# Layer 0 attention of a four-layer network: row normalisations, q and v's chunks in another order on VectorE and TensorE

## The reference

```
x = x + tanh(g_xattn[0]) * _L0_xattn_ref(_layernorm(x, axis=-1), ctx_1024, wq, bq, wk, bk, wv, bv, ln_g, ln_b, ...)

q = visual_tokens @ wq.T + bq
res = q
k = top_k_report_tokens @ wk.T + bk
v = top_k_report_tokens @ wv.T + bv
attn = softmax(einsum('bhqd,bhkd->bhqk', qh, kh) * d ** (-0.5), axis=-1)
out = einsum('bhqk,bhkd->bhqd', attn, vh)
out = _layernorm(res + out, ln_g, ln_b)
return _kan_linear(out, base_w, spline_w, spline_scaler, _grid())   # silu(out) @ base_w.T + b_splines(out) @ scaled_sw.T
```

## Time and profile before

| | us |
|---|---|
| median of 3 runs | 2769.6 (2768.28 to 2770.19) |
| the profiled execution, its own time | 2766.18 |
| its span in the trace, first to last instruction | 2764.4 |
| layer 0's attention stage ends at about | 412.9 |
| PE busy in the span | 2617.9 (95%) |
| DVE / ACT / POOL busy | 1547.1 / 1296.0 / 642.0 |

### The profile page before, as it was taken

The page is one execution under the profiler, slowest core; times in us unless marked ns, Lnnn a source line. Parts: engine busy times, 40 slices in busy tenths (PEclk is TensorE's granted clock), DMA queues, the critical chain, the costliest instruction groups (busy, mean ns, idle before and its releaser), DMA issues. The chain is left out here.

```text
span 2764.4 us, 56714 instructions
## 1 busy us (share of the span) xinstructions
PE 2617.9 (95%) x19818; PEld 1981.6 (72%) x19818; DVE 1547.1 (56%) x4177; ACT 1296.0 (47%) x3610; POOL 642.0 (23%) x626
## 2 busy tenths in 40 slices
PE   6999978999999999989899998999998999989998
PEld 4777756666666666656677766999995777768887
DVE  4777856555555555535787874333235887742222
ACT  4777743343434334331567663333335777732222
POOL 0666661000000000000444431222221111013232
PEclk9999989999999999999999999999999999999999
DMA  3000002000000000010000006999991000059897
GB/s 119 17 23 18 12 2 109 13 13 8 13 7 13 7 13 7 1 34 1 20 18 19 23 7 244 324 334 327 323 326 46 24 18 24 7 201 312 303 312 224
DMA packets 91811, 267.57 MB, mean 97 GB/s; under 512 B 25068, under 2 KB 50804, under 8 KB 77268
## 3 DMA queue, kind: packets, MB, share of 16 engines
q1 hardware_dynamic: 74356, 242.53, 25.4%
q0 software_dynamic: 13632, 18.62, 3.2%
q10 hardware_dynamic: 3616, 3.67, 0.4%
HBM read 248.13 MB, written 16.65 MB: 96 GB/s over the span
## 5 line engine op out<-in xcount | busy, mean ns | idle before, releaser
L825 PEld LDWEIGHTS a_full_ps<-ident,a_probs 112*125 112x125 f32 x2688 | 369.9, 190 | 122.6 <-issue 59.8
L1926 PEld LDWEIGHTS m_banks<-m_x_inT,m_w 128*128 128x128 f32 x3824 | 435.1, 192 | 15.2 <-issue 13.5
L1926 PE MATMUL m_banks<-m_x_inT,m_w 128*128 128x128 f32 x3824 | 442.2, 276 | 1.4 <-ACT m_x_inT L1997 0.9
L936 ACT ACTIVATE a_probs<-a_masked,a_negmax 112x375 f32<-112x375 f32 x512 | 305.4, 598 | 287.7 <-DVE a_negmax L1151 287.7
L825 PE MATMUL a_full_ps<-ident,a_probs 112*125 112x112 f32 x2688 | 417.5, 281 | 16.7 <-ACT a_pT L943 5.6
L1177 DVE COPY a_pT<-a_full_ps 125x448 f32<-125x448 f32 x448 | 277.4, 621 | 233.9 <-PE a_full_ps L825 231.9
L725 PE MATMUL a_full_ps<-attention_room 128*125 128x256 f32 (+1 forms) x960 | 330.0, 472 | 9.6 <-ACT a_qT L926 3.7
L717 PE MATMUL a_full_ps<-attention_room 128*128 128x375 f32 x896 | 325.0, 491 | 13.8 <-PEq L1769 8.6
L1151 DVE CUSTOM_DVE_ANT_0 a_masked<-a_sc_ps,a_mask_add 112x375 f32<-112x375 f32 x512 | 249.7, 544 | 33.2 <-PE a_sc_ps L812 32.0
L936 ACT ACTIVATE a_probs<-a_sc_ps,a_negmax 112x375 f32<-112x375 f32 x384 | 216.6, 575 | 89.4 <-DVE a_negmax L1157 89.3
L843 PEld LDWEIGHTS a_o_ps<-a_pT,a_v 125*32 125x32 f32 (+1 forms) x5376 | 165.2, 118 | 127.0 <-issue 98.7
(11 more groups left out here) (253 smaller groups left out, 3473.3 us busy)
## 6 DMA issues: line engine op xcount, KB each, us to landing
m_w<-in_L2f_w SPq DMA_DIRECT2D x105, 1024.0 KB, 6.4
m_w<-in_L3f_w SPq DMA_DIRECT2D x72, 768.0 KB, 5.9
attention_room<-in_ctxT SPq DMA_DIRECT2D x64, 375.0 KB, 3.1
m_w<-in_L3f_w SPq DMA_DIRECT2D x36, 640.0 KB
m_b<-in_L2f_b SPq DMA_DIRECT2D x35, 128.0 KB, 8.0
p_rows<-normed SPq DMA_DIRECT2D x16, 224.0 KB, 6.2
attention_room<-in_L0x_spline_wT SPq DMA_DIRECT2D x1, 2048.0 KB, 10.5
net_room<-in_L1f_w SPq DMA_DIRECT2D x2, 1024.0 KB
```

Source lines behind the costliest of these rows:

```text
L825: mm = pe.transpose(full_ps[0:KT, bank_of["turn", i, k], (j % 4) * S:(j % 4 + 1) * S], probs[:, i % 2, a, t * KT:(t + 1) * KT], ident[0:S, ...
L936: act.activation(probs[:, i % 2, a, 0:SK], src, ACT.Exp, bias=negmax[:, m:m + 1], scale=-1.0 if mask else 1.0, accum_out=rowsum[:, par, n: ...
L1926: mm = pe.matmul(ab_ps[:, (par * FC + f) % RING, i * SLOTS:(i + 1) * SLOTS], w[:, par, c, f * P:(f + 1) * P], x_inT[:, c, :], start=(c == ...
```

## The change

Only layer 0's attention stage changes, and there only orders; no instruction is added or removed. (1) In the table, q stands directly behind k, ahead of turn 1, and so in the bank of xT; (2) `rest` stands ahead of v's second chunk, and qtok last: v's second and third chunk get the banks of `lnt` and of turn 2, and qtok that of `kan`. (3) On VectorE resn stands in front of silu and the maxima, and the variance in front of the copy of turn 2. (4) `norm_apply`, `net_settle` and `norm_net.apply` stand between `norm_stats` and `update`.

```diff
 CYCLES = {
-    0: [[[("xT",)], [("k", 0)], [("q", 0), ("oback",)], [("v", 0, 0), ("k", 1)]],
-        [[], [], [("kan",), ("lnt",)], [("v", 1, 0), ("qtok",), ("v", 2, 0), ("rest",)]]],
+    0: [[[("xT",)], [("k", 0), ("q", 0)], [("oback",)], [("v", 0, 0), ("k", 1)]],
+        [[], [], [("kan",), ("lnt",)], [("rest",), ("v", 1, 0), ("v", 2, 0), ("qtok",)]]],
...
                         kan_residual(t - 1)
+                    if exists(t - 1):
+                        kan_variance(t - 1, 1 - par)
                     if exists(t):
                         copy_turn(t, 0, 2)
-                    if exists(t - 1):
-                        kan_variance(t - 1, 1 - par)
                     if exists(t - 2):
                         kan_cube(t - 2, 1)
+                    if exists(t - 1):
+                        kan_early(t - 1, 1 - par, 1)
+                    if exists(t - 2):
                         kan_silu(t - 2)
-                    if early(t - 3):
-                        net_settle(t - 3)
                     for group in ahead(t, par, 1):
                         row_max(*group)
-                    if exists(t - 1):
-                        kan_early(t - 1, 1 - par, 1)
...
                         norm_stats(t + 2)
+                    if early(t - 3):
+                        net_settle(t - 3)
+                    if exists(t + 2):
+                        norm_apply(t + 2)
+                    if early(t - 3):
+                        norm_net.apply(dve, t - 3, t - 3)
                     if exists(t - 2):
                         update(t - 2, full_ps[:, bank_of[("kan",)], :])
                     if exists(t):
                         copy_turn(t, 1, 2)
-                    if exists(t + 2):
-                        norm_apply(t + 2)
                     copies(t, par, 1, 3)
                     if exists(t - 2):
                         row_stats(t - 2)
-                    if early(t - 3):
-                        norm_net.apply(dve, t - 3, t - 3)
```

## The result

In ten runs of each on one chip the changed kernel took 2776.36 us (2770.38 to 2777.81), the kernel before 2770.09 (2768.28 to 2771.67): a ratio of 1.0021, 95% interval 1.0011 to 1.0030. It is slower, by 6.3 us or 0.2%; the forecast was 9.3. The profiled execution of the changed kernel took 2777.27 us, its span 2775.4, 11.0 more than the span of before. That is more than the 6.3 of the medians, since the profiled execution of before (2766.18) was quicker than each of the ten that give its median.

What follows compares the result with a forecast made beforehand. A VectorE and GpSimd cycle of 22.17 us a turn, over TensorE's 21.26, was to bind the changed kernel; 0.75 + 5.3 + 1.4 + 1.95 - 0.1 = +9.3 on 2769.6 gave 2778.9 us, range 2766 to 2786.

Steps and rivals of the forecast that it cites:

- The full turn: Full turns: a VectorE and GpSimd cycle of 22.17 us, 0.48 more than before, giving +5.3 over 12 turns.
- they take SBUF at 175.79 ... and the square is held until 176.26: Lines 1080 and 195 hold GpSimd's square, making its chain 0.33 us later; bounds 0 and 0.5.
- late resn: One turn before was 22.04 us long by a late resn; that 0.34 goes, leaving 5.3 of 5.8.
- q and v: TensorE's waits for q's copies and x's update shrink by 0.13 and 0.30, 0.43 us a turn, to 21.26.
- New waits: TensorE waits some 0.9 us a turn, before pv and silu's product; the late copy gives back about 0.12 at v's third chunk.
- The start: Turn 0: the copy of turn 2 comes behind line 1080 and v's third chunk waits: +0.75 us, bounds 0 and 1.1.
- Turn 15: pv waits for a copy that now follows held line 1211 and the variance: +1.4 us, bounds 0.5 to 2.
- Turn 16: Silu stands behind a held resn, and with it TensorE's 778: +1.95 us, bounds 0 to 2.2.
- Turn 17: One norm less stands in front of the cubes: -0.1 us.
- (c): Rival: `add_bases` gets SBUF between resn and silu, holding silu; +24 us more, 2803; chance 0.06.
- (a): Rival: TensorE stays the bound, the chain has unseen slack; sum -1.5 us, 2768.1, no change; chance 0.27.
- (d): Rival: the 0.9 us waits cost TensorE its clock in many turns; 9 us more, 2788; chance 0.06.

Runs made afterwards that it cites:

- e10_short_cube: Kernel before with the change's new table, VectorE's old order, and GpSimd's cube of near2's second half cut to one element: turn 21.77 us, ratio 0.9994.
- e16_before_act_square: Kernel before with ScalarE instead of GpSimd making the square of near2's second half: turn 21.71 us, ratio 1.0004.
- e13_after_short_cube: Changed kernel with GpSimd's cube of near2's second half cut to one element: turn 21.24 us, ratio 0.9979.
- e14_act_square: Changed kernel with ScalarE instead of GpSimd making the square of near2's second half: turn 21.24 us, ratio 0.9997.
- e15_act_square_tail: Changed kernel with ScalarE making the square of near2's second half, and VectorE's old order in turns 15 to 17: turn 21.24 us, ratio 0.9984.
- e1_table: Kernel before with only the change's new table, VectorE's order as before: turn 21.78 us, ratio 1.0014.
- e4_norms_back: Changed kernel with lines 1080 and 195 put back behind the update: turn 21.77 us, ratio 1.0006.
- e3_norms_only: Changed kernel with copy, variance, silu, maxima and resn back in the old order; new table and norms ahead stay: turn 21.78 us, ratio 1.0013.
- e2_vector: Changed kernel with the old table, VectorE's order the new one: turn 21.88 us, ratio 1.0025.
- e7_delay: Kernel before with two fills of unread buffers on VectorE behind layer 0's attention stage: median +7.9 us, ratio 1.0022.

## Why the forecast was right in sign and wrong in its parts

**What binds.** Right, for the changed kernel: a loop of VectorE and GpSimd over the held line 1211, with TensorE alone at 21.26 (shown: 21.24). Not seen: in VectorE's old order a second loop, over turn 2, the variance and resn, is at 21.7 to 21.8, and GpSimd's squares and cubes aren't in it (e10_short_cube, e16_before_act_square). In the kernel of before itself it lies so near TensorE's own work with its two waits that no run tells the two apart.

**The full turn.** The sum of the loop, in its rows: from lnT to the end of the second 629 12.85 (180.82 + 2.08 - 170.05), cube + 0.95, `add_bases` 0.20 later and 2.08 long, line 1211 + 0.28, and 5.51 to the next lnT: 21.87. In rows 3 and 4 the same steps are 12.77, 0.94, 0.21, 2.08, 0.31 and 5.38: 21.69. The forecast had put 0.33 on the first of them, where 0.08 came, and 0.18 on the last, where 0.13 came. The step that failed is "they take SBUF at 175.79 ... and the square is held until 176.26". The row at 196.32 shows the opposite, line 1080 held through the square. The 0.08 come with the first 629, at 2.24 in place of 2.10. Ten turns at 0.18, one of 21.24 (turn 2 to 3) and one of 22.19 give the 1.48. The one long turn, which I had put down to a late resn and taken off, is there in every kernel, 0.3 over the others, resn late or not. (The forecast's own sum slipped too: 12 x 0.48 less 0.34 is 5.4, not 5.3.)

**q and v.** q's copies start 13.91 us behind lnT (183.96 - 170.05), where the earlier trace rows have 14.82, 0.9 earlier and not 0.55. The sum of 0.43 was right, but it came out only in e13_after_short_cube, e14_act_square and e15_act_square_tail, where nothing else is in the way: 21.70 to 21.24. In e1_table both were given back at once, in a wait for resn.

**New waits.** Before pv and silu's product none came in full turns. The wait of v's third chunk for the copy of turn 2 did, at 0.45 and not 0.12: the held line 1080 stands ahead of that copy. TensorE loses its time there instead of before pv; with the norms back (e4_norms_back) it is 0.41 before pv.

**The start.** +0.75 can't be confirmed: v's third chunk waits 0.9 us for the copy in turn 0, as forecast, but the profiles of equal code differ by more.

**Turn 15.** The chain was right: line 1211 held, then variance, copy, and pv at 362.64 in place of 360.30. The size wasn't, and lies under its bound of 0.5: silu's product took 1.19 us, near the 1.03 of full clock, where it had taken 1.99, and the wait of 0.28 for resn before `lnt` fell away, so that +0.28 is left. **Turn 16** came as described: resn held for 2.15 with silu behind it, 778 at 386.27, +2.30 for 1.95; with silu ahead of resn again (e3_norms_only) the turn is 19.24, as before. **Turn 17** was wrong in sign (+0.77): two cubes took 4.86 in place of 2.08 and silu 2.25 in place of 0.38. The changed kernel and e3_norms_only, with the norms ahead and the new table, have this; e1_table and e2_vector, with one of the two, haven't; why VectorE loses SBUF between the cubes stays open.

**Rivals.** (c), a held silu, didn't come in full turns, but did in turn 17: `add_bases` had asked at 401.17, silu a microsecond later. The Trainium skill, SBUF — State Buffer, section "Who interferes with whom", has it that issue order decides who blocks, and this place of the trace agrees. The full turns don't: there `add_bases` asked at 189.35, silu's row begins at 189.39, and silu kept its 0.38. (a), a steady turn of 21.3, came in no kernel with GpSimd's full chain. (d), the clock lost inside the full turns, didn't come (1.00).

**The whole.** The forecast of +9.3 us for +6.3 is better than its parts, and that is luck. In the profiles the stage gave 3.9 of the 9.3, and 7.1 more came from the clock of stages that the change doesn't touch. No step of mine had that, though e7_delay shows that 3.7 us of delay are enough for it. How the 6.3 of the medians divide between the two isn't shown: each kernel has one profile.

## What to carry to other kernels

When a wait of the busiest engine is removed, follow both loops that close over it, not only the engine's own sum: here two loops within 0.1 us of each other gave all of it back in the full turns, and the same edit paid as soon as the other loop was shortened (0.45 us a turn together, none apart). Take a change of order out of the last turns, where there is no next turn's work to fill a wait (2.4 us here, in turns 15 and 16). And before a few microseconds are put down to an edit, compare the same instructions behind the stage: a mere delay of 3.7 us moved this kernel by 7.9.

## What the runs showed of the hardware

**Who gets SBUF isn't settled.** Where VectorE and GpSimd both want it at the end of an instruction, line 1080 (asked at 196.32) lost to the square that began at 196.77, right behind GpSimd's own line 188. In turn 17 GpSimd's 629 came between two cubes of VectorE, while at the same place before VectorE kept it over cube, cube and silu. Neither "who asked first" nor "who has it keeps it" fits all three. The experiments leave open what decides.

**An instruction can be held through two of the other engine**: 2.28 us for line 1080, which takes 0.41 alone.

**ScalarE isn't in this lock.** In e15 it makes the moved square, 128 x 896, in 0.93 us (at 176.07) beside GpSimd's two cubes, which take 4.31 together; in the changed kernel they take 2.24 and 2.08. GpSimd needs 1.68 for the square.

**The half clock of TensorE depends on when a stretch comes.** The thirteen kernels of the table, whose later stages have the same code (in the two with the short cube on other values), differ by -0.3 to +7.2 us behind layer 0's attention against the profile of before (table, end less stage), with no order in the size of the shift: +2.9 brought 6.3 more, +3.1 brought 2.5. What makes the stretches fall otherwise isn't shown.
